# Attention over 16 heads: score banks by block of queries, maxima subtracted in 64-row tiles, masked keys dropped in the values

## The reference, cut to what matters

```python
kv_input = jnp.concatenate([x, lat], axis=1)          # 256 context rows, 256 latents
kv_mask = jnp.concatenate([masks, jnp.ones((b, q_len), dtype=bool)], axis=1)
...
sim = jnp.einsum('bhqd,bhfd->bhqf', q, k)
sim = sim - jax.lax.stop_gradient(jnp.max(sim, axis=-1, keepdims=True))
sim = jnp.where(kv_mask, sim, -jnp.inf)
alphas = jax.nn.softmax(sim, axis=-1)
out = jnp.einsum('bhqf,bhfd->bhqd', alphas, v)
out = out.transpose(0, 2, 1, 3).reshape(b, q_len, INNER)
return out @ Wo
```

## Time and profile before

| what | value |
|---|---|
| median of 3 runs | 764.87 us |
| runs | 764.4, 764.87, 769.9 us |
| span of the profiled execution | 761.9 us |
| median less span | 3.0 us |
| PE busy | 610.9 us (80%) |
| DVE busy | 569.0 us (75%) |
| POOL busy | 417.5 us (55%) |
| ACT busy | 324.3 us (43%) |

### The profile page before, as it was taken

How to read it: one execution, slowest core, us unless ns; L and a number is a source line. 1 busy time by engine, 2 the same in 40 slices (tenths; PEclk the granted TensorE clock), 3 DMA queues, 4 the chain that set the end, 5 groups by cost and what they waited for, 6 DMA issues and landing times.

```text
span 761.9 us, 15577 instructions
## 1 busy us (share of the span) xinstructions
PE 610.9 (80%) x5721; PEld 387.8 (51%) x5721; DVE 569.0 (75%) x1043; ACT 324.3 (43%) x565; POOL 417.5 (55%) x349
## 2 busy tenths in 40 slices
PE   6399756798468658838428899999999998799997
PEld 5277522354244335325313456666666665566766
DVE  4837899659969985995976777667667766489887
ACT  2433200231132132113213787767858766455661
POOL 5424254417636652769593756656656666346652
PEclk9999977769779858965556999999999999989999
DMA  7311100000000000003310000000000000000001
GB/s 190 90 34 29 55 1 0 0 2 1 0 2 0 0 0 0 0 0 97 96 28 0 2 2 2 2 2 2 2 2 2 2 2 2 1 1 0 0 0 28
DMA packets 14163, 12.95 MB, mean 17 GB/s; under 512 B 3120, under 2 KB 11936, under 8 KB 14112
## 3 DMA queue, kind: packets, MB, share of 16 engines
q1 hardware_dynamic: 14112, 12.25, 5.6%
HBM read 11.72 MB, written 0.52 MB: 16 GB/s over the span
## 4 chain that ended last, share of the span: by engine, by line
PE 57%; DVE 28%; issue 7%; ACT 3%; POOL 3%; DVEq 1%; DMA 1%; ACTq 0%; SPq 0%; POOLq 0%; PEld 0%
DVE work L717 5%; PE banks L1034 5%; PE banks L1712 5%; DVE work L775 4%; PE banks L1041 4%; PE banks L950 3%; PE banks L465 3%; PE banks L1059 3%; PE banks L1019 2%; PE banks L952 2%; PE banks L951 2%; PE banks L1067 2%; PE banks L1422 2%; PE banks L1061 2%; PE banks L1060 2%
## 5 line engine op out<-in xcount | busy, mean ns | idle before, releaser
L1361 POOL TENSOR_TENSOR attn<-work,attn 128x512 f16<-128x512 f32 (+1 forms) x96 | 141.9, 1481 | 94.8 <-ACT attn L1160 94.8
L1250 DVE TENSOR_REDUCE nmax<-banks 128x2 bf16<-128x1024 f32 x64 | 78.3, 1223 | 21.5 <-PE banks L1019 21.3
L717 DVE TENSOR_TENSOR work<-banks,gatev 128x512 f32<-128x512 f32 x120 | 79.3, 684 | 15.8 <-PE banks L467 15.3
L465 PE MATMUL banks<-weights,xbTh 128*128 128x512 f16 x120 | 50.7, 422 | 28.2 <-DVE work L717 26.7
L1469 POOL TENSOR_SCALAR work<-work 128x512 f16<-128x512 f32 x64 | 53.0, 851 | 35.7 <-ACT work L1401 33.1
L1159 ACT ACTIVATE work<-banks,maskbias 128x512 f32<-128x512 f32 x64 | 44.3, 692 | 59.7 <-PE banks L1041 59.7
L845 POOL TENSOR_TENSOR work<-work 128x512 f32<-128x512 f32 x24 | 30.5, 1269 | 66.6 <-DVE work L717 64.6
L1407 DVE TENSOR_TENSOR work<-work 128x512 f16<-128x512 f32 x64 | 57.1, 949 | 12.2 <-POOL work L1469 12.2
L1712 PE MATMUL banks<-ident,work 128*128 128x128 f32 x276 | 53.3, 331 | 8.5 <-DVE work L1912 3.0
L490 PE MATMUL banks<-attn 64*128 64x256 f16 x64 | 22.1, 360 | 47.0 <-ACT work L631 37.9
L1059 PEld LDWEIGHTS banks<-work,attn 128*128 128x128 f16 x512 | 46.8, 97 | 18.8 <-POOL attn L1361 10.8
(11 more groups left out here) (275 smaller groups left out, 1922.2 us busy)
## 6 DMA issues: line engine op xcount, KB each, us to landing
stage<-in_L_ffn_w SPq DMA_DIRECT2D x8, 512.0 KB, 3.9
stage<-in_L_ffn_Wkv SPq DMA_DIRECT2D x4, 640.0 KB, 3.9
stage<-in_L_ffn_Wq SPq DMA_DIRECT2D x2, 640.0 KB, 5.1
xt<-in_x SPq DMA_DIRECT2D x1, 512.0 KB, 4.2
ct<-in_ctx SPq DMA_DIRECT2D x1, 512.0 KB, 5.5
wo<-in_L_xattn_Wo SPq DMA_DIRECT2D x1, 512.0 KB
stage<-in_L_xattn_Wv SPq DMA_DIRECT2D x1, 512.0 KB, 3.7
stage<-in_L_xattn_Wq SPq DMA_DIRECT2D x1, 512.0 KB, 3.5
```

The lines of the kernel that those rows point to most:

```text
L465: pe.matmul(o, xh, wh, start=True, stop=False)
L717: dve.tensor_tensor(heads8(m.prod[:, k, e, :]), heads8(bank_pj[c % 2][:, :]), wide(g, DH1), ALU.mult).then_inc(s.prod_ready, 1)
L1250: dve.tensor_reduce(m.nmax[:, p % 2, i, :], banks[:, 6:8, :], AX.X, ALU.max, negate=True).then_inc(s.c_max_done, 1)
L1361: pool.tensor_tensor(m.Pl[:, p % 2, kts, :], m.Pf[:, kts, :], m.Ph[:, p % 2, kts, :], ALU.subtract).then_inc(s.c_P_lo, 1)
```

## The change

Each score bank now belongs to one head and one block of 128 queries, with all four key tiles: `scores_T(t, i)` makes 24 matmuls of 128 columns where there were 12 of 256. The maxima are subtracted by four matmuls of 64 rows, two for each half of the block's queries; for the head whose rows are not those of the queries, DVE moves the maxima to the other 64 partitions first (`move_max`, two copies of 64x2 to `nmoved`), and TensorE waits for that with a semaphore of its own. The exponentials of a pair are two groups of 1024 columns instead of two of 512 and one of 1024, none with a bias; POOL subtracts in two pieces of 1024. Masked keys are dropped by multiplying the values, and the column of ones that gives the sum, by the mask (an extra small ACT copy, and a per-partition scale in ACT and DVE) for key tiles 0 and 1. The bias copies and their waits are gone.

```diff
-            def scores_T(it, p, half):
+            def scores_T(it, p, i):
 
                 if p >= 1:
-                    pe.wait_ge(s.c_exp_done, it * EXPS + (3 * (p - 1) + 2 + half))
...
+                    pe.wait_ge(s.c_exp_done, it * PAIRS + (I * (p - 1) + i + 1))
+                pair = [bank[:, :].rearrange("p (k c) -> p k c", k=KT) for bank in bank_kq[2 * i:2 * i + 2]]
+                for kt in range(KT):
                     for x in range(3):
                         for h in range(2):
                             r = slice(DH2 * h, DH2 * h + DH2)
                             key = (m.k2h, m.k2l, m.k2h)[x][r, p % 2, kt * P:(kt + 1) * P]
-                            q = (m.q2h, m.q2h, m.q2l)[x][r, p % 4, :]
-                            pe.matmul(pair[h][:, k * S:(k + 1) * S], key, q, start=(k == 0 and x == 0), stop=False)
-                if half == 0:
-                    pe.wait_ge(s.c_max_done, it * PAIRS + (2 * p + 2))
-                for h in range(2):
-                    o = pair[h][:, :].rearrange("p (k i c) -> p k i c", k=2, i=I)
-                    for i in range(I):
-                        less = m.nmax[:, p % 2, i, h:h + 1].to_broadcast([P, P])
-                        ins = pe.matmul(o[:, :, i, :], less, m.identb[:, :].unsqueeze(1).to_broadcast([P, 2, P]), start=False, stop=(i == I - 1))
+                            q = (m.q2h, m.q2h, m.q2l)[x][r, p % 4, i * P:(i + 1) * P]
+                            pe.matmul(pair[h][:, kt, :], key, q, start=(kt == 0 and x == 0), stop=False)
+                if i == 0:
+                    pe.wait_ge(s.c_max_moved, it * HP2 + (p + 1))
+                for high in range(2):
+                    for h in range(2):
+                        r, at = slice(DH2 * h, DH2 * h + DH2), slice(DH2 * high, DH2 * high + DH2)
+                        less = (m.nmax[r, p % 2, i, h:h + 1] if h == high else m.nmoved[r, p % 2, i:i + 1]).to_broadcast([DH2, P])
+                        one = m.identb[r, r].unsqueeze(1).to_broadcast([DH2, KT, DH2])
+                        ins = pe.matmul(pair[h][:, :, at], less, one, start=False, stop=(high == 1))
                 ins.then_inc(s.c_S_ready, 1)
...
+                    if j[2] < I:
+                        valid = m.maskcol[:, it + j[1], j[2]:j[2] + 1]
+                        act.activation(m.v2h[:, j[2], j[3] * 8:j[3] * 8 + 8, DH2], valid.to_broadcast([P, 8]), ACT.Copy)
+                        act.activation(dst, src, ACT.Copy, scale=valid).then_inc(s.c_pj_hi, 1)
+                        return
...
+            def exps(it, p, i):
+
+                act.wait_ge(s.c_S_ready, it * PAIRS + (I * p + i + 1))
                 if p >= 1:
...
+                    act.wait_ge(s.c_P_lo, it * PAIRS + (I * (p - 1) + i + 1))
+                scores = banks[:, 2 + 2 * i:4 + 2 * i, :]
+                act.activation(m.Pf[:, i, :, :, :].rearrange("p h k c -> p h (k c)"), scores, ACT.Exp, scale=DH2 ** -0.5)
+                act.activation(m.Ph[:, p % 2, i, :, :], scores, ACT.Exp, scale=DH2 ** -0.5).then_inc(s.c_exp_done, 1)
...
+            def move_max(it, p):
+
+                dve.wait_ge(s.c_max_done, it * PAIRS + (2 * p + 2))
+                low, high = slice(0, DH2), slice(DH2, P)
+                dve.tensor_copy(m.nmoved[low, p % 2, :], m.nmax[high, p % 2, :, 0])
+                dve.tensor_copy(m.nmoved[high, p % 2, :], m.nmax[low, p % 2, :, 1]).then_inc(s.c_max_moved, 1)
...
                 if more:
                     take_max(it, t + 1, 1)
+                    move_max(it, t + 1)
...
+                for i in range(I):
+                    pool.wait_ge(s.c_exp_done, it * PAIRS + (I * p + i + 1))
+                    low, full, high = m.Pl[:, p % 2, i, :, :], m.Pf[:, i, :, :, :], m.Ph[:, p % 2, i, :, :]
+                    low, high = (a.rearrange("p h c -> p (h c)") for a in (low, high))
+                    pool.tensor_tensor(low, full.rearrange("p h k c -> p (h k c)"), high, ALU.subtract).then_inc(s.c_P_lo, 1)
```

More of the change, by code:

```diff
@@ L238, in build @@
               *((PT_AT + k * 512, (2, 4, P), F16) for k in range(2)),
-              *((k * KT * 512, (2, KT, 512), F16) for k in range(2)))
+              *((k * KT * 512, (2, I, 2, KT * P), F16) for k in range(2)))
         m.den = sb("den", [P, 8])
@@ L1144, in high @@
                 act.activation(dst, src, ACT.Copy).then_inc(s.c_pj_hi, 1)
-            def exps(it, p, r):
-                act.wait_ge(s.c_S_ready, it * PAIRS + (2 * p + r // 2 + 1))
+            def exps(it, p, i):
+                act.wait_ge(s.c_S_ready, it * PAIRS + (I * p + i + 1))
                 if p >= 1:
[L1150 to L1159, removed]
-                act.activation(hi, src, ACT.Exp, scale=DH2 ** -0.5, bias=bias).then_inc(s.c_exp_done, 1)
+                    act.wait_ge(s.c_P_lo, it * PAIRS + (I * (p - 1) + i + 1))
+                scores = banks[:, 2 + 2 * i:4 + 2 * i, :]
+                act.activation(m.Pf[:, i, :, :, :].rearrange("p h k c -> p h (k c)"), scores, ACT.Exp, scale=DH2 ** -0.5)
+                act.activation(m.Ph[:, p % 2, i, :, :], scores, ACT.Exp, scale=DH2 ** -0.5).then_inc(s.c_exp_done, 1)
             def step(it, t):
@@ L1238, in low @@
                     v = (slice(None), j[2], slice(j[3] * 8, j[3] * 8 + 8), slice(0, DH2))
-                    ins = dve.tensor_tensor(m.v2l[v], heads2(bank[:, :]), m.v2h[v], ALU.subtract)
+                    if j[2] < I:
+                        valid = m.maskcol[:, it + j[1], j[2]:j[2] + 1]
+                        ins = dve.scalar_tensor_tensor(m.v2l[v], heads2(bank[:, :]), valid, m.v2h[v], ALU.mult, ALU.subtract)
+                    else:
+                        ins = dve.tensor_tensor(m.v2l[v], heads2(bank[:, :]), m.v2h[v], ALU.subtract)
                 elif kind == "k":
@@ L1357, in low_exps @@
             def low_exps(it, p):
-                for r in range(3):
-                    kts = slice(r, r + 1) if r < 2 else slice(2, 4)
-                    pool.wait_ge(s.c_exp_done, it * EXPS + (3 * p + r + 1))
-                    pool.tensor_tensor(m.Pl[:, p % 2, kts, :], m.Pf[:, kts, :], m.Ph[:, p % 2, kts, :], ALU.subtract).then_inc(s.c_P_lo, 1)
+                for i in range(I):
[3 more added lines that the diff above has]
+                    pool.tensor_tensor(low, full.rearrange("p h k c -> p (h k c)"), high, ALU.subtract).then_inc(s.c_P_lo, 1)
             for t in range(SPLIT_AT):
```

30 lines of the change are left out of this document (10 added, 20 removed).

## The result

| | median | runs | ratio to before, 95% |
|---|---|---|---|
| before | 764.63 us | 4, 764.02 to 769.9 | |
| after | 775.5 us | 4, 771.88 to 775.99 | 1.0148 [1.0119, 1.0177] |

The change makes the kernel 10.9 us slower, by 1.5%. 770 and no difference beyond 1% were forecast. The profiled execution took 775.79 us, its span is 774.1.

A forecast was written before the change was run, and what follows sets the result against it. TensorE was taken as full in mid-attention, with DVE's maxima finishing just as needed. Held moves in the middle +3.5, first steps +1.1, end +0.5 made +5 us on the 764.87 median: 770, range 752 to 776.

The forecast's parts named there:

- TensorE's part: Attention's half steps: score pairs every 0.055 us, no mode-change gaps around subtractions, a half from 1.30 to 0.89.
- one rival's second price: Unheld moves with scores at 0.061 us a pair: 755.5 us instead of 753; the unheld rival had 0.25.
- the two steps without a hold: Middle of attention, moves not held: query step stays 7.05 us, gaining nothing; the other 6.01 against 6.84.
- the moves are held: Forecast's main case, 0.60 (766 to 776): DVE's copies wait for POOL's ops, TensorE's next subtractions lose 0.88 us.
- the rival of 753: Moves not held by POOL: a pair takes 13.06 us, the kernel 753 (750 to 757); chance 0.25.
- the exposed weight loads: Rival: 64-row weight loads not hidden, score pairs above 0.09 us, kernel about 778 us; chance 0.05.
- +0.28: Loss per pair taken in the middle, between +0.05 (one blocked move) and +0.45 (both); +3.5 us over some 12.5 pairs.
- just inside the query step's longer chain: After the short step's held moves, key's low half, outputs and first maximum come late but fit within that chain.
- the tie that the prediction named: Query step: POOL's second op starts at 5.41, moves ready at 5.40; if lost, the short step loses about 1.1 us.
- the masked values cost the attention nothing: Masked value copies stand at the end of ACT's step, covered; at most 10 us if that cover were gone.
- At the end the last moves are held too, +1.0, less 0.5: End of the attention: held last moves cost 1.0 us, shorter last exponentials give back 0.5.
- the first steps, +1.1: First steps, paced by DVE's other work: earlier key copy gives 0.9, moves held in two cost 1.0 each.

The follow-up runs named there:

- moves_as_maxima: The changed kernel with its two copies of each step written as maxima over one element, same place in VectorE's order: 758.89 us, 0.995 of before.
- maxima_q_between: The changed kernel with moves as maxima and, in query steps, ScalarE's query copy between the first pair's two exponentials: 747.86 us, 0.9809 of before.
- full_rows: The changed kernel with the subtraction in 128 rows, one matmul of 512 columns per head, and no moves: 772.51 us, 1.0129 of before.
- before_masked_values: The kernel before with only masked keys dropped in the values and their ones, and no bias in the exponentials: 758.69 us, 0.9955 of before.
- maxima_at_edges: The changed kernel with moves as maxima in the first five and last steps, copies in the middle loop: 764.97 us, 1.0022 of before.
- no_moves: The changed kernel without the moves, subtracting wrong maxima (the same rows' other head) instead: 758.28 us, 0.9935 of before.
- moves_on_act: The changed kernel with the two moves on ScalarE, behind the step's second pair of exponentials: 761.9 us, 0.9993 of before.
- low_in_halves: The changed kernel with GpSimd's subtraction of 1024 columns as two of 512, copies as they are: 764.83 us, 1.0043 of before.

## Why the prediction was wrong, point by point

**Right: TensorE's part.** Pairs every 0.055, no time lost around the subtractions, halves of 0.90. (The 0.061 a pair of one rival's second price stands in no run.)

**Right: the two steps without a hold.** 6.04 and 7.08 in moves_as_maxima, where 6.01 and 7.05 were worked out; and that the query step gains nothing because of the query copy, which maxima_q_between shows by moving it. full_rows shows the same term without the gain of the 64-row subtractions, +0.35 a query step. The rival's time for this case, 753, was wrong all the same: moves_as_maxima took 758.9, outside its 750 to 757, because the ends cost what they cost there too (below).

**Right: the moves are held; what that costs in the middle came out near by luck.** The copies end with GpSimd's pieces as forecast, the rival of 753 is out, and so are the exposed weight loads. A pair went from 13.90 to 14.15, +0.25, where +0.28 was taken; over steps 4 to 29 +1.9 where +3.5 stood. But the +0.28 was chosen between two states, +0.05 where one step of the pair is blocked and +0.45 where both are. Once the steps have settled, both copies of the short step are held and those of the query step not at all (0.17 each): the state priced at +0.05, which cost +0.25. The wait for the subtraction is 0.57, less than the 0.88 forecast; 0.97 more comes by what is queued behind the copies, of which the prediction said "just inside the query step's longer chain". In steps 4 to 9 the query step's second copy alone was held, the tie that the prediction named, and the pair took the same 14.15. Both were blocked in one pair alone (steps 10 and 11), between these two states.

**Right: the masked values cost the attention nothing** (before_masked_values).

**Wrong: "At the end the last moves are held too, +1.0, less 0.5".** This term of +0.5 measured +10.0: +4.3 from step 30 on, +1.2 in the projections, +4.5 behind the attention. The held copies of the last short step make the whole row of VectorE's work in step 30 late by about 2 us (its second maximum ends 5.64 us into that step before, 7.72 after). TensorE idles meanwhile, its clock falls to the 1.2 GHz level, and the rest of the step, the last scores, the projections and the start of the next stage run in part at that level. The prediction had no term for the clock at all, and that is the step that failed: 2 us of the 10 are the delay, and the rest lies where the clock is at that level. Of the 4.5 behind the attention, 1.2 stand in the first 10 us of the next stage, and 3.2 in the last 15 us of the kernel, over a hundred us behind the last held copy: there TensorE waits 2.25 us for VectorE, as it did before (2.24), but its last matmuls run at 0.50 (763 to 767 us), where before they ran at 1.00.

How much of that rest the held copies cause isn't shown, and for the last 3.2 us nothing ties it to them. With no held copies at the ends, maxima_at_edges takes 125.4 us from step 30 on, less than the 126.0 before; but no_moves, moves_as_maxima and moves_on_act, without any, take 130.4, 133.7 and 134.1, against 136.0 in the kernel after. Part of TensorE's idle time comes from the shorter half steps alone: in step 30, where VectorE's two maxima are due, it waits 1.80 and 1.41 us in all the kernels named, against 1.08 and 1.41 before, and 1.06 and 1.41 in full_rows, which has no 64-row subtractions. The held copies add the 0.57 and 0.97 ahead of that.

**Wrong in size: the first steps, +1.1.** They measured +3.5. With maxima instead of copies +1.4 is left, so up to 2.1 are held copies: three, of 1.99, 2.00 and 2.15 us, where two were counted at half a GpSimd op. The rest isn't settled, but the clock, again without a term, goes with part of it: no_moves, where nothing is moved, has 32.7 us there; its step 2 takes 9.60 us where moves_as_maxima has 8.14, and the granted clock of 430 to 434 us is 0.57.

**Open.** Why the clock falls at the end in one kernel and not in another. moves_as_maxima has the same last steps as maxima_at_edges and no hold, and lost 6.8 us by the measure above where the other lost 3.4, though TensorE was idle for the same time in both. Windows of moves_as_maxima, then of maxima_at_edges:

```profile
623.00:625.00 2.00, 0.47 (x14) 1.00 0.00 0
625.00:627.00 2.00, 0.39 (x2) 1.00 0.00 0
...
629.00:631.00 2.00, 2.00 (x32) 0.50 0.04 8
```

```profile
641.00:643.00 2.00, 0.45 (x13) 1.00 0.00 0
643.00:645.00 2.00, 0.39 (x2) 1.00 0.00 0
...
647.00:649.00 2.00, 2.00 (x52) 1.00 0.03 8
```

And the 3.2 us by which the kernel after reached the attention earlier came with another granted clock in an earlier stage, 0.80 against 0.69 in 250 to 300 us, where the change does nothing that these runs tell apart.

The sum, then: 3.5 + 1.9 + 4.3 + 1.2 + 4.5 = 15.4, less 3.2 ahead of the attention, where 1.1 + 3.5 + 0.5 was forecast. The 3.2 stand in no term; without them 770 would have been further off.

## What to carry to other kernels

A copy that is tiny in bytes is not tiny in time when GpSimd works beside it: price it at the piece that GpSimd is in, and at everything queued behind the copy; writing it as a reduction over one element takes the price away, and cutting GpSimd's op in halves took most of it (a pair of 13.30, where 13.12 is the price of nothing held). When a half step gets shorter, look at which copy on ScalarE still stands behind longer work, for the gain can hide behind one order of two instructions, as the query copy here. At the end of a stage, where TensorE idles for some microseconds, it can come back at half its clock; here two kernels with the same last steps and no held copies there were 8 us apart from step 30 on, with the granted clock at 0.50 in different stretches. Sum up the ends of a loop separately, look at the granted clock behind them, and give the term a range.

## What the runs showed of the hardware that wasn't expected

- A held copy gets in between two pieces of GpSimd that stand without a gap, but only one copy does at each boundary: of two copies in a row the first took 0.90 and the second 2.07 us (after), with half pieces 1.04 and 1.10 (low_in_halves).
- The same maxima, two elements a partition, moved by a reduction over one element took 0.15 us in all 64 cases, and by ScalarE 0.20; in either kernel GpSimd was at work during 62 of the 64.
- Equal code at the end of a stage, behind equal idle time of TensorE, ran once at granted clock 1.00 (maxima_at_edges, 639 to 667) and once with 0.50 for some microseconds (moves_as_maxima, 629 to 631 and 639 to 645), with the rest of the span 102.9 and 107.7 us long.
